# Attention layer on one core: weighted values directly behind the scores, the linear piece last

## The reference, cut to what matters

```python
x = x + attention(layernorm(x))     # rotary q and k, ALiBi on earlier tokens only, softmax, output projection
x = x + ffn(layernorm(x))           # base = x @ W.T + b, correction = (x @ V_r) @ C.T
# attention, per head:  attn = q @ k.T * SCALE + alibi;  w = softmax(attn);  out = w @ v
```

## Time and profile before

| | |
|---|---|
| profiled execution | 2117.53 us, its span 2115.4 us |
| timed executions, median (range) | 2112.39 us (2108.58 to 2112.86) |
| PE busy | 2080.8 us, 98% of the span |
| DVE busy | 1858.1 us, 88% |
| ACT busy | 1513.2 us, 72% |
| POOL busy | 1297.1 us, 61% |
| granted TensorE clock, mean | 0.984 |

### The profile page before, as it was taken

How to read it: one execution, slowest core, us unless ns; L and a number is a source line. 1 busy time by engine, 2 the same in 40 slices (tenths; PEclk the granted TensorE clock), 3 DMA queues, 4 the chain that set the end, 5 groups by cost and what they waited for, 6 DMA issues and landing times.

```text
span 2115.4 us, 81946 instructions
## 1 busy us (share of the span) xinstructions
PE 2080.8 (98%) x33596; PEld 1195.8 (57%) x33596; DVE 1858.1 (88%) x5459; ACT 1513.2 (72%) x2562; POOL 1297.1 (61%) x1093
## 2 busy tenths in 40 slices
PE   5999999999999999999999999999999999999998
PEld 3455555555555555555555555555555555555554
DVE  8799998998998998999899999899899999899962
ACT  2377777777777777777777777777778777777663
POOL 6457565666666666756666756566666666666512
PEclk8799999999999999999999999999999999999998
DMA  6233334333334334333334333433333433433311
GB/s 176 73 114 103 94 103 111 108 113 106 101 95 123 104 105 123 102 88 111 104 113 115 103 94 103 115 104 113 107 99 97 123 96 113 118 106 87 102 34 36
DMA packets 158887, 218.78 MB, mean 103 GB/s; under 512 B 19024, under 2 KB 104912, under 8 KB 158512
## 3 DMA queue, kind: packets, MB, share of 16 engines
q1 hardware_dynamic: 157232, 211.44, 35.4%
q10 hardware_dynamic: 1280, 2.10, 0.3%
HBM read 36.52 MB, written 16.78 MB: 25 GB/s over the span
## 4 chain that ended last, share of the span: by engine, by line
PE 91%; DVE 1%; ACT 1%; issue 1%; POOL 0%; DVEq 0%
PE ps_s L434 29%; PE ps_o L457 21%; PE ps_misc L413 18%; PE ps_misc L400 12%; PE ps_misc L387 3%; PE ps_misc L476 3%; PE ps_t L444 3%; PE ps_misc L467 2%; DVE junk L646 1%; ACT pt L835 0%; PE ps_t L517 0%; ACT x_res L783 0%; ACT x_res L778 0%; DVE x_hat L679 0%; DVE x_res L631 0%
## 5 line engine op out<-in xcount | busy, mean ns | idle before, releaser
L646 DVE CUSTOM_DVE_ANT_0 junk<-ps_s,alibi 128x512 bf16<-128x512 f32 x2004 | 1302.7, 687 | 183.4 <-PE ps_s L434 152.4
L835 ACT ACTIVATE pt<-ps_t 128x1024 f32<-128x1024 f32 x1024 | 1049.5, 1025 | 453.0 <-DVE ps_t L656 444.8
L444 PE MATMUL ps_t<-at 64*128 64x512 f32 x2048 | 764.9, 452 | 2.0 <-ACT pt L835 2.0
L434 PE MATMUL ps_s<-at 64*128 64x512 f32 x2004 | 755.9, 454 | 1.9 <-DVE row_max L646 1.2
L457 PE MATMUL ps_o<-pt,v_one 128*17 128x128 f32 x16384 | 640.8, 274 | 1.4 <-ACT pt L835 1.3
L457 PEld LDWEIGHTS ps_o<-pt,v_one 128*17 128x17 f32 x16384 | 442.3, 98 | 186.5 <-issue 45.4
L434 PEld LDWEIGHTS ps_s<-at 64*128 64x128 f32 x2004 | 325.3, 184 | 239.0 <-DVE row_max L646 132.2
L656 DVE TENSOR_TENSOR ps_t<-ps_t,diag 128x256 f32<-128x256 f32 x1024 | 435.4, 425 | 21.7 <-PE ps_t L444 21.5
L1001 POOL TENSOR_TENSOR rope_b<-raw,rope_sin 128x512 f32<-128x512 f32 x128 | 164.6, 1286 | 333.9 <-ACT raw L815 327.5
L1017 POOL TENSOR_TENSOR halves<-rope_a,swapped 128x512 fp32r<-128x512 f32 x126 | 159.4, 1287 | 313.1 <-DMA swapped<-rope_b 313.1
L444 PEld LDWEIGHTS ps_t<-at 64*128 64x128 f32 x2048 | 329.5, 185 | 14.7 <-ACT pt L835 7.1
(11 more groups left out here) (105 smaller groups left out, 1801.5 us busy)
## 6 DMA issues: line engine op xcount, KB each, us to landing
at<-halves SPq DMA_DIRECT2D x192, 512.0 KB, 3.9
swapped<-rope_b SPq DMA_DIRECT2D x256, 128.0 KB, 2.6
x_in<-in_L_attn_x_dram SPq DMA_DIRECT2D x32, 512.0 KB, 5.4
num<-o_sb SPq DMA_DIRECT2D x512, 32.0 KB, 2.0
x_res<-in_L_attn_x_dram SPq DMA_DIRECT2D x32, 512.0 KB, 4.4
out_dram<-x_hat SPq DMA_DIRECT2D x32, 512.0 KB, 5.9
at<-spread_den SPq DMA_DIRECT2D x60, 64.0 KB
at<-max_t ACTq DMA_DIRECT2D x128, 16.0 KB
```

Source lines behind the costliest of these rows:

```text
L434: pe.matmul(scores_bank(n, t), operand(n, 0)[:, t * P:(t + 1) * P], operand(n, 1), start=True, stop=True).then_inc(s_done, 1)
L444: pe.matmul(ps_t[:, j, :], operand(n, 1)[:, j * P:(j + 1) * P], operand(n, 0), start=True, stop=True).then_inc(t_done, 1)
L646: dve.tensor_tensor_reduce(unused, scores_bank(n, t), alibi[:, off:off + N], 1.0, LOWEST, ALU.add, ALU.max, row_max[:, hb % 2, t, hh:hh + ...
L835: act.activation(pt[:, h % 2, 2 * pair:2 * pair + 2, :], ps_t[:, 2 * pair:2 * pair + 2, :], ACT.Exp).then_inc(exp_done, 1)
```

## The change

In each half, the two calls of `weighted_values` move from behind everything else to directly behind the scores. The pieces (linear, turning, spreading, maxima) now come last. Nothing is added or removed, and the programs of the other engines are the same.

```diff
@@ -540,6 +540,9 @@
                             max_scores(n, t)
                         if nt is not None:
                             exp_scores(nt, t)
+                    if nv is not None:
+                        weighted_values(nv, 2 * half)
+                        weighted_values(nv, 2 * half + 1)
                     for u in range(2):
                         b, quarters = due(now, *V[u])
                         for quarter in quarters:
@@ -577,9 +580,6 @@
                             spread_denominators(b, kc)
                     if hb is not None and half == 1:
                         max_rows(hb)
-                    if nv is not None:
-                        weighted_values(nv, 2 * half)
-                        weighted_values(nv, 2 * half + 1)
```

## The result

The changed kernel takes 2207.77 us (median of 4, 2204.62 to 2210.78), the kernel before beside it 2110.48 us (median of 4, 2102.62 to 2112.86). The ratio is 1.0458, with a 95% interval of 1.0431 to 1.0486: 97 us slower, where 99 were forecast. The profiled execution has a span of 2208.8 us against 2115.4, 93.4 more.

A forecast was written before the change was run, and what follows sets the result against it. The prediction took PE's own work, busy 98% at full clock, as the bound. Its waits, 56 us for the ps_o copy and 43 for DVE's chain, sum to +99, median 2112.39 to 2211; range 2154 to 2264.

The forecast's parts named there:

- What bounds the kernel, and the sum: PE's own work sets the time at full clock; the added waits make +99 us, median 2112.39 to 2211.
- PE's own work: Same instructions and handovers on PE, 2.11 us a half as before; taken as 0, bounds -20 to +30 us.
- (a): Group starts: the values wait 0.66 or 0.59 us for ACT's ps_o copy, queued behind emptying the bank; 56 us.
- (b): Six halves a batch where DVE empties the bank: bias, exponential and the next scores come late; 1.39 a batch, 43 us.
- (c): ACT's other copies, such as the v copy of half 27, move later but are covered: 0, 5 us if thin.
- The clock rival: The granted clock falls once a batch for two halves: 105 us more, 2316; chance 0.10.
- only DVE's chain acts: Rival: the ps_o copy is not in the way, only the late exponentials cost: 2112 + 43 = 2155; chance 0.08.
- the order doesn't change: Rival: the order on the engine stays as before the edit, 2112; chance 0.02.
- The rival on the fast side: Handover to the scores: weight loads hide behind a long piece, up to 0.11 us a half; 2098; chance 0.04.

The follow-up runs named there:

- experiment 1: The changed kernel with ACT copying ps_o ahead of emptying the bank: 2153.86 us, ratio 1.0206 to the kernel before.
- experiment 3: The changed kernel with ACT's ps_o copy ahead of emptying the bank and DVE's diagonal bias directly behind the row maxima: 2103.13 us, ratio 0.9973 to the kernel before.

## Why the prediction was right

**What bounds the kernel, and the sum.** Right. PE sets the pace before and after, at the full clock, and the loss is PE waiting. Forecast +99 us, measured +97, and +93 between the two profiled executions. A batch lasted 62.74 us before (start of half 31 to the next, 1036.02 to 1098.76) and lasts 65.81 now (1080.22 to 1146.03), 3.07 more, times 31 is 95; over 30 batches the mean is 3.01 more, times 31 is 93.

**PE's own work.** Forecast as unchanged with a gain of 0.02 a half as one bound; it is a small gain. A full half of the changed kernel, on PE:

```profile
1088.97 0.49 PE L434 MATMUL ps_s<-at 64*128 64x512 f32 x1
...
1089.63 0.63 PE L457 MATMUL ps_o<-pt,v_one 128*17 128x128 f32 x16
1090.08 1.05 PE L413 MATMUL ps_misc<-proj_t,attn_t 128*32 128x256 f32 x16
```

Scores to values 0.66, values to piece 0.45, piece to the next scores (1091.06) 0.98: 2.09, against 2.11 and 2.10 before. The handover that no row had shown, values to piece, costs next to nothing for a linear piece; to a turning it takes 0.57 (1117.38 to 1117.95), which the turning gives back behind it. Its size for the run follows from the batch: the parts below lose 1.86 + 1.39 + 0.23 = 3.48 us in each, and the batch got 3.07 longer, so PE gained 0.4 in 32 halves, 12 us in all. That is within the bound and was not in the sum.

**(a) The copy of ps_o.** Right in place, mechanism and sum: 91 waits forecast, 90 seen; 56 us forecast, 54 came back when ACT's order was turned, and the lateness of the values against S + 0.66, summed over these 90 starts in the trace, is 55.5. The single waits are not where the sum had them: 0.58 behind xt, where it had 0.66, and 0.63 and 0.65 behind x2t and a q or k piece, where it had 0.59. These errors cancel, which is luck. One comes from the reading of the earlier trace rows: the 0.55 taken for emptying the bank held a wait of ACT, whose next copy, at 1054.51, starts 0.07 behind the recorded end of the values it needs (1053.81 + 0.63). Without that wait the two copies start 0.49 apart (1099.62 to 1100.11).

**(b) DVE's chain.** Right as well: 43 us forecast, 46 came back (42 by the batch). Single places: 0.19 behind halves 3, 19 and 21 where 0.16 was put, since the chain takes 2.28 and the half 2.09; 0.18 behind half 31 where 0.15 was put; 0.46 behind half 5, of which 0.09 was lost before, so the 0.37 of the text; behind half 0 0.27 more than before rather than 0.39. That 0.39 was too much by the wait at the start of half 1, which PE has already spent by then and which the sum counts by itself. On the other side DVE is still busy with a row maximum there and starts the divide at S + 0.20, not 0.14, and the product comes at S + 2.33. The parts as measured make 1.39 a batch, the same as the sum, so here too errors cancel.

**(c) ACT's other copies.** This step failed: a term put at 0, with a bound of 5 us, measured 7. Timeline of the changed kernel, ACT and PE: v copy, squares and exponential of half 27, and the scores that open half 29:

```profile
1074.49 0.59 ACT L791 COPY v_one<-ps_misc 128x512 f32<-128x512 f32 x1 [0.96 <-PE ps_misc L413]
...
1074.97 0.51 ACT L772 ACTIVATE x_hat<-x_in,minus_mean 128x256 f32<-128x256 f32 x1
...
1075.47 1.01 ACT L835 ACTIVATE pt<-ps_t 128x1024 f32<-128x1024 f32 x1
...
1076.44 0.50 PE L434 MATMUL ps_s<-at 64*128 64x512 f32 x1
...
1076.54 0.50 PE L444 MATMUL ps_t<-at 64*128 64x512 f32 x1
```

S of half 28 is 1074.35. The v copy starts at S + 0.14, the squares behind it, and the exponential only at S + 1.12; it ends at 1076.48 and the product that needs it starts at 1076.54, 0.10 late. I had looked at the next exponential, which the 0.55 of the earlier trace rows does cover, and not at this one, which gates half 29 itself; 0.14 + 0.48 + 0.50 + 1.02 + 0.05 against a half of 2.09 would have shown it. In the batches with a usual course the products that open halves 29, 30 and 31 start 0.11, 0.14 and 0.15 late (1142.48 to 1142.59, 1144.24 to 1144.38, 1146.03 to 1146.18), before 0.00, 0.07 and 0.10: 0.23 more, times 31 is 7 us.

So the parts make 56 + 43 + 7 less some 12 on PE, 94 us: 97 were timed, and the batches give 93. The closeness of the total is partly luck: the small loss in (c) and the small gain on PE were both left out and partly cancel, on top of the errors within (a) and (b).

**The clock rival** did not come: PEclk shows 9 in all the slices of the body, and in a stretch of 2020 us of it the granted clock is 1.00. So the waits of half a microsecond that the change brings, the longest idle time of PE there being 0.58, did not bring the clock down. The rule that the prediction took from the Trainium skill (TensorE: Matmul & The Clock Gate, on why this matters for kernels), that PE have no long idle gap, held here: the clock stayed up. That it isn't a guarantee stays as the earlier trace rows have it.

**The rivals of sign and size.** That only DVE's chain acts (2155) is out by experiment 1; that the order doesn't change is out by the timeline. The rival on the fast side was wrong in its price, not wholly in its kind: the handover did get cheaper, by 0.01 to 0.02 a half and not by 0.11, and only with the two waits taken away does that show in the time. That the scores' weight loads are what got cheaper is not shown. Two numbers of the range have no working: its lower corner takes 45 us for (a), for which no row was given, and its upper end of 2264 lies 2 us above 2112 + 150.

## What to carry to other kernels

When one engine's work is reordered, the other engines' orders are part of the change: for each result that now comes later, look at what stands behind its consumer in that consumer's fixed order, and at who waits for that. Here nearly all of the 97 us hung on that, and moving one copy and one addition turned a loss of 4.6% into a gain of 0.2 to 0.3%, while the same two moves cost the kernel before 60 and 16 us. A cover of half a microsecond is worth a term of its own when the covered work itself moves.

## What the runs showed of the hardware

The release of a consumer by a matmul group was steadier than I had thought. In the changed kernel DVE started add_linear 0.14 behind the next scores in nearly all of the 30 recorded cases behind each of halves 3, 5, 19 and 21 (1091.06 to 1091.20, 1095.42 to 1095.56; the latest at 0.16). ACT started its copies at 0.11, 0.14 or 0.17, each value the same in every batch, where nothing else held it. So a chain of four handovers could be summed from rows to within 0.03 us where DVE was free (2.27 forecast, 2.28 measured), and was 0.06 off behind half 0, where it was not.

Also not expected: a 128x32 piece is recorded 0.02 us shorter behind the 17-column values than behind the scores (16 records take 1.05 instead of 1.07), and with scores behind it takes 0.98 from start to start instead of 1.00. And in experiment 3 the second scores of half 2 start at the usual S + 0.34 (1039.12), but their weights only with them, where the weights lead by 0.23 in half 3 (1041.09 to 1041.32); the values follow 0.44 later in the one and 0.32 in the other. That the late weight load is what costs the 0.12 is not shown by a run of its own.
